# A semaphore for each quarter of a load: four sums that wait for their own quarter only

## What is computed

```python
logits = jnp.einsum('bmd,dnp->bmnp', x, phi)
dispatch = jax.nn.softmax(logits, axis=0)
combine = jax.nn.softmax(logits.reshape(bsz, m, n * p), axis=-1).reshape(bsz, m, n, p)
slots = jnp.einsum('bmd,bmnp->bnpd', x, dispatch)
y = jnp.einsum('bnpd,nde->bnpe', slots, W) + b[None, :, None, :]
out = jnp.einsum('bnpd,bmnp->bmd', y, combine)
```

## Time and profile before

| | |
|---|---|
| time, median of 3 runs | 682.45 us (681.97 to 682.69) |
| time of the profiled execution | 680.64 us |
| its span, first to last instruction | 678.2 us |
| TensorE busy | 634.2 us, 94% |
| VectorE busy | 429.6 us, 63% |
| ScalarE busy | 364.9 us, 54% |
| GpSimd busy | 242.6 us, 36% |
| granted clock of TensorE, mean | 0.993 |

### The profile page before, as it was taken

The page is one execution under the profiler, slowest core; times in us unless marked ns, Lnnn a source line. Parts: engine busy times, 40 slices in busy tenths (PEclk is TensorE's granted clock), DMA queues, the critical chain, the costliest instruction groups (busy, mean ns, idle before and its releaser), DMA issues.

```text
span 678.2 us, 15044 instructions
## 1 busy us (share of the span) xinstructions
PE 634.2 (94%) x5329; PEld 394.4 (58%) x5329; DVE 429.6 (63%) x857; ACT 364.9 (54%) x710; POOL 242.6 (36%) x419
## 2 busy tenths in 40 slices
PE   5899999999999999999989986999999999999975
PEld 5788645444444444444444464777666666666664
DVE  5956998733322433353433789887888888887782
ACT  5656777742223333334443565766666666666661
POOL 5454787800000000000000083555554554554455
PEclk9999999999999999999999999999999999999999
DMA  8900021224444444443454211222222222222210
GB/s 277 397 29 0 1 78 48 63 76 132 129 130 132 132 131 131 131 132 117 133 159 136 92 43 64 93 85 85 85 84 76 82 82 83 82 82 80 83 40 32
DMA packets 73234, 68.66 MB, mean 101 GB/s; under 512 B 3185, under 2 KB 63602, under 8 KB 72946
## 3 DMA queue, kind: packets, MB, share of 16 engines
q1 hardware_dynamic: 70864, 66.07, 30.3%
q10 hardware_dynamic: 2338, 2.16, 0.9%
HBM read 43.32 MB, written 23.07 MB: 98 GB/s over the span
## 4 chain that ended last, share of the span: by engine, by line
PE 42%; DMA 24%; DVE 13%; SPq 6%; issue 5%; POOL 5%; ACT 4%; POOLq 0%; DVEq 0%; ACTq 0%
PE psL L1544 21%; DMA xx<-logit_difference 21%; PE psM L1531 10%; DVE r_xn L1266 4%; SPq L386 4%; PE psM L1561 3%; DMA logit_difference<-r 2%; POOL small L480 2%; DMA r_xn<-in_proj_wT 1%; PE psL L1431 1%; PE psM L1490 1%; SPq L427 1%; ACT r_xn L853 1%; PE psL L1490 1%; ACT r L853 1%
## 5 line engine op out<-in xcount | busy, mean ns | idle before, releaser
L1544 PE MATMUL psL<-r,r_xn 128*128 128x512 f16 x768 | 176.4, 379 | 0.8 <-DVE r L1088 0.8
L1544 PEld LDWEIGHTS psL<-r,r_xn 128*128 128x128 f16 x768 | 73.4, 98 | 91.6 <-issue 6.8
L1531 PE MATMUL psM<-phs,xx 128*128 128x512 f16 (+1 forms) x384 | 93.2, 379 | 0.0
L1086 DVE TENSOR_SCALAR r<-r 128x512 f16<-128x512 f32 x64 | 29.0, 453 | 98.7 <-ACT r L743 98.7
L567 POOL MEMSET r_xn<- 128x16 f16 x1 | 0.2, 174 | 237.3 <-PE psL L1544 237.3
L743 ACT ACTIVATE r<-psM,small 128x512 f32<-128x512 f32 x64 | 43.7, 682 | 72.8 <-PE psM L1531 72.0
L1663 PE MATMUL psL<-phs,r 128*32 128x512 f16 x1344 | 75.1, 379 | 1.0 <-DMA r<-xx 1.0
L1531 PEld LDWEIGHTS psM<-phs,xx 128*128 128x128 f16 x384 | 37.3, 98 | 44.7 <-issue 0.7
L1266 DVE CUSTOM_DVE_ANT_0 r_xn<-psL,xx 128x512 f32<-128x512 f32 x60 | 38.9, 686 | 33.4 <-DMA xx<-logit_difference 33.2
L480 POOL TENSOR_TENSOR small<-small,epst 128x2 f32<-128x2 f32 (+3 forms) x75 | 57.0, 760 | 6.2
L1663 PEld LDWEIGHTS psL<-phs,r 128*32 128x32 f16 x1344 | 34.6, 97 | 37.4 <-issue 2.8
(11 more groups left out here) (206 smaller groups left out, 1310.8 us busy)
## 6 DMA issues: line engine op xcount, KB each, us to landing
logit_difference<-r SPq DMA_DIRECT2D x64, 256.0 KB, 2.3
xx<-logit_difference SPq DMA_DIRECT2D x64, 256.0 KB
r<-in_ffn_w SPq DMA_DIRECT2D x15, 1024.0 KB, 5.4
out<-r SPq DMA_DIRECT2D x32, 128.0 KB, 2.2
xres<-in_x SPq DMA_DIRECT2D x7, 512.0 KB, 9.8
r<-in_phi SPq DMA_DIRECT2D x1, 2048.0 KB, 17.7
expert_bias<-r ACTq DMA_DIRECT2D x1, 2048.0 KB, 18.3
r<-expert_bias SPq DMA_DIRECT2D x16, 128.0 KB, 3.0
```

The costliest lines, as they stand in the source:

```text
L1086: own.add(V.tensor_scalar(thl[:, j % 2, 0], tF[:, j % 2], S_SCALE, None, ALU.mult))
L1531: ins = mm(bk[j % 2][:, :].rearrange("p (q m) -> p q m", q=EP), xxT[:, 1, j, hx, k, :], phw[:, hp, k, :, bass.ds(nb, 1), :].rearrange("p q ...
L1544: ins = mm(psL[:, i * 512:(i + 1) * 512], x3n[:, b, j, hx, k * P:(k + 1) * P], thl[:, j % 2, hs, :], start=(j == 0 and hx + hs == 0), stop ...
```

## The change

The semaphore dB_loaded becomes four, one for each quarter. Each of the four DMAs of `load_d` adds to its own. The single wait for all four quarters ahead of the first sum goes, in the loop and for tile 0, and `add_max` waits for the semaphore of its quarter, with `wait_apart`.

```diff
-        dB_loaded, x1_loaded = sem("dB_loaded"), sem("x1_loaded")
+        dB_loaded, x1_loaded = [sem(f"dB_loaded{g}") for g in range(GJ)], sem("x1_loaded")
...
-                                     "j q r m -> (j q) r m")).then_inc(dB_loaded, 16)
+                                     "j q r m -> (j q) r m")).then_inc(dB_loaded[g], 16)
...
             def add_max(j, g):
                 c = slice(512 * g, 512 * g + 512)
+                wait_apart(dve, dB_loaded[g], 16 * j + 16)
                 V.tensor_tensor_reduce(E0[:, c], logits_at(j)[:, c], dB[:, c], 1.0, -3.0e38, ALU.add, ALU.max,
                                        lmax[:, 1, g:g + 1]).then_inc(l_added, 1)
...
                 dve.wait_ge(ET_ready[0], 2 * j)
-                wait_apart(dve, dB_loaded, 64 * j + 64)
                 add_max(j, 0)
                 add_max(j, 1)
...
             mask1()
-            dve.wait_ge(dB_loaded, 64)
             for g in range(GJ):
                 add_max(0, g)
```

## The result

The changed kernel takes 666.42 us (median of 4 runs, 665.76 to 667.91), the kernel before 682.57 us in the same comparison: a ratio of 0.9767, with a 95% interval of 0.9747 to 0.9787. It is faster by 15.9 us, and the interval puts it at 665.3 to 668.0; the forecast was 667.6, its range 664.5 to 674. The two profiled executions took 680.64 and 665.8 us, which is 14.8 us, where 14.9 was the sum. The four runs of the changed kernel spread over 2.2 us, so an agreement within 0.1 us is in part luck.

A forecast was written before the change was run, and what follows sets the result against it. Loads bound the combine stage at 17.42 us a tile, then TensorE at 16.30. Saving 15.06 - 0.2 = 14.9 us takes the profiled 680.64 to 665.8, plus 1.81 to the median: 667.6 us, range 664.5 to 674.

The forecast's parts named there:

- The bound before: Combine stage: the loads of logit differences set 17.42 us a tile, while TensorE has 16.30 us of work in it.
- The landings: Four quarter loads of a tile are served one after the other, landing at about 588.3, 590.9, 593.5 and 596.1 us.
- The Trainium skill's remark: Rival of no gain, chance 0.06: quarters land together at the end, leaving 682.5 us; a later descriptor may finish first.
- The load's ring: Mask to last landing plus wake, 14.51 us, and fourth sum to mask, 0.73 us: 15.24 us a tile after the change.
- TensorE's 16.30 us: TensorE's own pace per combine tile, the bound after the change; the loop's last fold comes at 634.71 us, 12.64 us earlier.
- The stall of 1.1 us at the second fold: TensorE's wait for VectorE's mask at the other batch's maxima goes, with 1.4 us to spare.
- The tail: After the last fold, ScalarE's batch 0 exponentials come at 639.69 instead of 654.75 us: 15.06 us, including the loop's gain.
- The waits added: Four waits a tile on VectorE in place of one: free in the loop, 0.2 us once at the end.
- From the profile to the median: Median of the runs taken as 1.81 us above the profiled execution: 665.8 us becomes 667.6 us.
- ScalarE and GpSimd's ring: Rival, chance 0.14: this combine-stage cycle of 15.88 us, 0.42 under TensorE's pace, grows to 16.88 and gives 674 us.
- the 3.36 us from one set of exponentials to the other: ScalarE's time from batch 1's to batch 0's exponentials (424.32 to 427.68), a part of the 15.88 us cycle.
- The stretched instruction that the rival needed: GpSimd's L593, 1.56 us beside a VectorE subtraction and 0.56 elsewhere; such a 1.0 us could land on the 15.88 us cycle.

The follow-up runs named there:

- experiment 5: Four small copies (128 x 64) more on ScalarE at the end of each tile, against the changed kernel: 675.96 us; with one copy 666.8 us.
- experiment 1: Changed kernel, four semaphores kept, waits for later quarters moved: all ahead of first sum 682.64 us, from second on 673.35 us, last two ahead of third 665.3 us.

## Why the prediction was right

**The bound before.** The loads set 17.42 us and TensorE had 1.1 us a tile to spare. Shown: less work for TensorE changed nothing (0.9999), a shorter load gave the whole gain (0.9753).

**The landings.** Taken as one after the other from a flat rate. The reversed order gave the whole gain away (1.0002), and the counts on the semaphores show the spacing, 2.55 to 2.59 us. The Trainium skill's remark (DMA: Bandwidth & Descriptors, "Queues, rings and completion order") that a later transfer may finish its write first had no effect that shows here: in no tile of the changed kernel or of the one with the reversed order did a quarter's last count come ahead of that of the quarter issued before it.

**The load's ring, 15.24 us.** It is no more the bound, and its parts are confirmed from three sides: with the second and third sum behind the last landing as well, 16.80 us was expected, 16.84 measured, and the time came out at 673.35 for 673.5; with the first two sums free and the last two behind it, nothing was lost; with 1.5 us added to it, 670.45 for 671.

**TensorE's 16.30 us.** Measured 16.31 us, and the last fold at 634.84 for 634.71. The stall of 1.1 us at the second fold is gone in every tile.

**The tail.** From the last fold to the exponentials 639.86 - 634.84 = 5.02 us, where the sum had 0.44 + 4.54 + 0.2 = 5.18. The saving by this row is 654.75 - 639.86 = 14.89 us for 14.86.

**The waits added.** The one term that was sized too large. I took 0.2 us on the tail's path; from reduction to exponentials it is 574.63 - 570.05 = 4.58 us, 0.04 more than before. The waits ahead of the second and fourth sum are passed while the sum ahead of them runs, and the one ahead of the third, which follows the short bias, costs the 0.04. The one ahead of the first sum shows its 0.19 us, and the kernel before had that wait too. The last fold came 0.13 us later than forecast, and the two nearly cancel.

**From the profile to the median.** The forecast of the median took over the 1.81 us by which the median before lay above its profiled execution. For the changed kernel that distance is 0.6 us. This is the scatter between executions, and it is why the median gained 16.2 us and the profile 14.8. The miss of the median, 667.6 for 666.42, comes from here.

**The rival that came closest** is ScalarE and GpSimd's ring. The prediction gave it 0.42 us to spare. The run with four copies gives 0.6, and the ring that came next when TensorE was relieved, with VectorE in it, had 0.35 (16.31 against 15.96). The term that was off is the 3.36 us from one set of exponentials to the other, "where nothing delayed them": VectorE's bias ahead of the second set took 0.42 us there, 0.23 elsewhere, beside GpSimd's L593, which ran from 427.06 to 427.62 us. With the 3.19 us of experiment 5 the prediction's sum would be 15.71 us. VectorE's row in the kernel before:

```profile
427.22 0.42 DVE L1274 TENSOR_SCALAR small<-small 128x4 f32<-128x4 f32 x1
```

The stretched instruction that the rival needed did move. GpSimd's groups in the combine loop, 440 to 640 us, first before the change and then after:

```profile
L593 POOL TENSOR_SCALAR r<-r,small 128x256 f32<-128x256 f32 x23 | 20.4, 885 | 4.9 <-POOL small L591 4.9
...
L589 POOL TENSOR_TENSOR small<-small 128x1 f32<-128x1 f32 x23 | 4.4, 192 | 1.8
```

```profile
L589 POOL TENSOR_TENSOR small<-small 128x1 f32<-128x1 f32 x25 | 15.9, 635 | 2.0
L593 POOL TENSOR_SCALAR r<-r,small 128x256 f32<-128x256 f32 x25 | 14.0, 559 | 5.3 <-POOL small L591 5.3
```

The delay that L593 had beside VectorE's subtraction now falls on L589. It is the same finish of batch 0, which is not on the ring, so it cost nothing.

## What to carry to other kernels

A wait in a ring costs only what the ring exceeds the next one by: here 2.6 us of waiting a tile was worth 1.1, since the neighbour's work was 16.3 of 17.4 us. One takes the pace of that neighbour from a tile in which it did not wait, and the size of the gain follows before anything is built. When several transfers feed several uses, what counts is how many uses stand behind the last landing and that transfers are issued in the order of use; past the point where the next engine is full, further splitting brings nothing. And the chain that ended last can name a group of engines that has slack, if its ring runs only a few tenths under the true bound. Its share of "issue" doesn't tell the two apart: it was 27.2% where TensorE was the bound and 22.7% with fewer matmuls, where it was not. Taking a little work from one side and adding a little to the other does.

## What the runs showed of the hardware

Four transfers of 262 KB, issued one after the other on one queue within 2.9 us, landed 2.55 to 2.59 us apart in the order of issue, also when that order was reversed (the combine stage from the tile at 421 us on, in these two kernels and the one before). A sum that waited for such a landing started 0.18 us after the last count on its semaphore, in each of the last 13 tiles of the kernel before.

A wait as an instruction of its own, with an increment, costs VectorE nothing where a sum of 0.6 us runs ahead of it and its semaphore has been reached: second sums start 0.61 us after the first with it (568.18 - 567.57) and without it (569.23 - 568.62, the kernel with halved loads). Behind the short bias it costs a little: from the reduction to the third sum it is 0.34 us before the change, 0.38 with one wait and 0.49 with two (experiment 1, all ahead of the third sum).

In one profile TensorE's mean granted clock was lower in the combine stage. In the kernel before with fewer matmuls it was 0.94, most of the time at the level of 2.4 GHz and for the rest at 1.2, with 2.2 us of waiting a tile. The stretch from 400 us to the end:

```profile
400.00:682.00 282.00, 238.58 (x2670) 167.75 (x2668) 223.31 (x399) 177.67 (x336) 147.20 (x233) 0.94 0.21 74
```

From 480 to 620 us it is 0.95 there. It is 1.00 in that stretch in the kernel before (1.2 us of waiting a tile), in the changed kernel (none) and in the changed kernel with fewer matmuls (1.4 us). The time did not feel it, as the loads were the bound; that the waiting brought it about is not shown.

A small VectorE instruction can be held up by GpSimd: in the run with four more copies on ScalarE the bias of the exponent, 0.23 us in the changed kernel, took 1.15 us, as it took 1.16 in the run with fewer matmuls. It ended at 574.91, and GpSimd's subtraction of the low halves beside it (L572 before) at 574.89. VectorE's row and GpSimd's:

```profile
573.76 1.15 DVE L1282 TENSOR_SCALAR small<-small 128x4 f32<-128x4 f32 x1
```

```profile
572.76 2.13 POOL L574 TENSOR_TENSOR r<-xx,r 128x1024 f16<-128x1024 f32 x1
```
